# Value tiles turned by SBUF-to-SBUF DMAs and VectorE's 32x32 transposes instead of by TensorE: a gated-delta attention layer with an expert FFN on one core

## The reference, cut to what matters

```python
mixed = hidden_states @ W_qkv
mixed = _causal_conv_silu(mixed.transpose(0, 2, 1), conv_w).transpose(0, 2, 1)
q, k, v = jnp.split(mixed, [KEY_DIM, 2 * KEY_DIM], axis=-1)
...
def step(S, inp):
    qt, kt, vt, gt, bt = inp
    S = S * jnp.exp(gt)[..., None, None]
    v_adj = (vt - jnp.einsum('bhk,bhkv->bhv', kt, S)) * bt[..., None]
    S = S + kt[..., None] * v_adj[..., None, :]
    o = jnp.einsum('bhk,bhkv->bhv', qt, S)
    return (S, o)
```

## Time and profile before

| | us |
|---|---|
| median of 3 runs | 2076.18 |
| lowest and highest | 2070.57, 2081.19 |
| the profiled execution's own time | 2080.1 |
| its span in the trace | 2078.3 |

### The profile page before, as it was taken

One profiled execution on the slowest core, in us unless ns is written; L12 is line 12 of the kernel. 1 busy time (PEld: TensorE's weight loads), 2 busy tenths in 40 slices (PEclk: granted clock), 3 DMA queues, 4 the chain that ended last, 5 costly groups with the idle time before them and its releaser, 6 DMA issues.

```text
span 2078.3 us, 39559 instructions
## 1 busy us (share of the span) xinstructions
PE 2008.6 (97%) x13730; PEld 1713.5 (82%) x13730; DVE 1353.6 (65%) x3169; ACT 909.1 (44%) x2525; POOL 834.1 (40%) x2123
## 2 busy tenths in 40 slices
PE   5789999999999999999999999999999999999999
PEld 3578888888888888888888888888888888887887
DVE  6868877778688878787777445555555444446442
ACT  4555555555465555556555532222223232233221
POOL 1456666666575766666565511100010210101111
PEclk9889999999999999999999999999999999999999
DMA  4233545343535444434443232443334434303441
GB/s 125 51 74 79 97 84 100 79 96 80 89 84 94 92 97 81 97 81 97 88 87 71 77 93 59 94 92 81 77 76 92 118 86 99 69 26 122 152 143 70
DMA packets 388022, 184.25 MB, mean 89 GB/s; under 512 B 249456, under 2 KB 369136, under 8 KB 385776
## 3 DMA queue, kind: packets, MB, share of 16 engines
q1 hardware_dynamic: 354640, 177.73, 37.8%
q10 hardware_dynamic: 33184, 4.01, 1.3%
HBM read 135.26 MB, written 46.40 MB: 87 GB/s over the span
## 4 chain that ended last, share of the span: by engine, by line
PE 69%; issue 10%; DVE 6%; DMA 5%; POOL 4%; ACT 3%; SPq 2%; ACTq 0%; POOLq 0%; DVEq 0%
PE bank L333 17%; PE bank L335 17%; PE bank L334 17%; DMA VT<-v_dram 4%; PE bank L565 3%; PE bank L574 2%; PE bank L548 2%; PE bank L468 2%; PE bank L584 2%; PE bank L556 2%; PE bank L527 2%; PE bank L533 1%; POOL y_out L1823 1%; POOL V L1771 1%; POOL prod L1769 1%
## 5 line engine op out<-in xcount | busy, mean ns | idle before, releaser
L1769 POOL TENSOR_TENSOR prod<-A_in,V 128x60 f32<-128x60 f32 (+24 forms) x992 | 301.4, 304 | 269.6 <-DMA A_in<-a_dram 199.3
L1771 POOL TENSOR_TENSOR V<-V,prod 128x60 f32<-128x60 f32 (+24 forms) x992 | 311.1, 314 | 77.8
L1098 ACT ACTIVATE hid<-bank,bias 128x512 f32<-128x512 f32 x128 | 88.3, 690 | 455.3 <-PE bank L335 453.5
L1813 POOL TENSOR_TENSOR ffn_w_lo<-ffn_raw,ffn_w_hi 128x1024 fp32r<-128x1024 f32 x32 | 77.9, 2437 | 470.3 <-ACT ffn_w_hi L1088 466.4
L1563 DVE TENSOR_TENSOR h_lo<-hid,h_hi 128x512 fp32r<-128x512 f32 x128 | 91.1, 712 | 265.8 <-ACT h_hi L1105 265.8
L1577 DVE SCALAR_TENSOR_TENSOR gate_acc<-bank,rw,gate_acc 128x512 f32<-128x512 f32 x240 | 177.6, 748 | 58.8 <-PE bank L335 58.8
L333 PE MATMUL bank<-ffn_w_hi,h_hi 128*128 128x512 f32 x512 | 199.3, 389 | 1.2 <-DVE h_lo L1563 1.0
L333 PE MATMUL bank<-xn_hi,ffn_w_hi 128*128 128x512 f32 x512 | 200.3, 391 | 0.0
L335 PE MATMUL bank<-xn_hi,ffn_w_lo 128*128 128x512 f32 x512 | 199.2, 389 | 0.0
L334 PE MATMUL bank<-xn_lo,ffn_w_hi 128*128 128x512 f32 x512 | 199.2, 389 | 0.0
L335 PE MATMUL bank<-ffn_w_hi,h_lo 128*128 128x512 f32 x512 | 199.2, 389 | 0.0
(11 more groups left out here) (224 smaller groups left out, 5178.0 us busy)
## 6 DMA issues: line engine op xcount, KB each, us to landing
E<-eg_dram SPq DMA_DIRECT2D x64, 256.0 KB, 8.1
A_in<-a_dram SPq DMA_DIRECT2D x32, 512.0 KB, 4.0
decb<-dec_dram SPq DMA_DIRECT2D x128, 128.0 KB, 4.2
og_dram<-og SPq DMA_DIRECT2D x64, 256.0 KB, 2.2
ffn_raw<-w SPq DMA_DIRECT2D x32, 512.0 KB, 4.0
og_x<-og_dram SPq DMA_DIRECT2D x256, 64.0 KB, 2.7
ogT_dram<-og_y SPq DMA_DIRECT2D x64, 256.0 KB, 2.4
og_in<-ogT_dram SPq DMA_DIRECT2D x16, 1024.0 KB, 5.2
```

The source lines that it names most:

```text
L1098: act.activation(hid[:, i % 2, :], bank[i % 4][:, :], ACT.Gelu_apprx_tanh, bias=bias1[:, k, f * NF + ft:f * NF + ft + 1]).then_inc(S_["gel ...
L1769: pool.tensor_tensor(prod[:, 0:m, 0:n], column, V[:, vb, 0:m, j:j + 1].to_broadcast([P, m, n]), MUL).then_inc(S_["product"], 1)
L1771: pool.tensor_tensor(V[:, vb, 0:m, j + 1:B32], V[:, vb, 0:m, j + 1:B32], prod[:, 0:m, 0:n], ADD).then_inc(S_["solve_step"], 1)
L1813: pool.tensor_tensor(fw[m, "lo", n % 2][:, :], raw[:, i % 2, :], fw[m, "hi", n % 2][:, :].bitcast(f32), SUB).then_inc(S_["ffn_lo"], 1)
```

## The change

TensorE no longer turns the values. `turn_v` on PE (8 transposes in a block) is gone. In its place:

- SP has a new `load_v`, at the end of a step behind its last `decb` load: once both silu tiles of the block are there and the block before has been turned, it issues 16 DMAs from `vS` to a new tile `v_x`, each of 32 partitions x 8 pieces of 32 elements (32 KB). They put the 32x32 blocks of every 128x128 tile at their transposed places.
- DVE has a new `turn_v`: two transposes of 128x512 in 32x32 blocks, from `v_x` to `v_tok`, between `chain_S` of chunk 3 and `convolve(st, "v0")`.
- ACT's `put_v` scales `v_tok` in place. Its two halves move from the middle of the step to its end, around `put_y64`.
- `v_tok` has one buffer instead of two; `v_x` takes the room of the other.
- PE's waits change: `turn_k` waits for what `turn_v(st, 0)` waited for, and `project_v0` waits for the third z gate of the block and no longer for `v_tok`.
- ACT's four carry semaphores become one, each wait still being for its own instruction just before.

```diff
@@ PE
             def project_v0(st):
                 if is_block(st - 1):
-                    pe.wait_ge(S_["v_tok"], 2 * st)
+                    pe.wait_ge(S_["z_gate"], CPS * (st - 1) + 3)
...
             def turn_k(st):
                 b = st - 1
-                pe.wait_ge(S_["v_tok"], 2 * b + 1)
+                if is_block(st):
+                    pe.wait_ge(S_["CP"], CPS * (st + 1))
+                else:
+                    pe.wait_ge(S_["k_rem"], b)
...
@@ PE, attention_step
                     chain_out(st - 2, 1)
-                if turned:
-                    turn_v(st, 0)
...
                 if turned:
-                    turn_v(st, 1)
                     turn_k(st)
@@ ACT
             def put_v(st, half):
                 b = st - 1
-                act.wait_ge(S_["v_turned"], 2 * b + half + 1)
+                act.wait_ge(S_["v_turned"], b + 1)
...
-                    r = act.mul(v_tok[:, b % 2, c, :], TV_BANK[half][:, i * REP * HD:(i + 1) * REP * HD], roots[:, b % 4, c:c + 1])
+                    r = act.mul(v_tok[:, :, c, :], v_tok[:, :, c, :], roots[:, b % 4, c:c + 1])
...
@@ ACT, end of attention_step
                 if turned:
+                    put_v(st, 0)
                     put_y64(st - 1)
+                    put_v(st, 1)
@@ DVE
+            def turn_v(b):
+                dve.wait_ge(S_["v_x"], V_X * (b + 1))
+                if b:
+                    dve.wait_ge(S_["R"], CPS * b)
+                for h in range(REP):
+                    r = dve.transpose(v_tok[:, h, :, :], v_x[:, h * CPS:(h + 1) * CPS, :])
+                r.then_inc(S_["v_turned"], 1)
...
                 if chain:
                     chain_S(st - 2, 3)
+                if turned:
+                    turn_v(st - 1)
                 if now:
                     convolve(st, "v0")
@@ SP
+            def load_v(b):
+                sp.wait_ge(S_["act_v0"], b + 1)
+                sp.wait_ge(S_["act_v1"], b + 1)
+                if b:
+                    sp.wait_ge(S_["v_turned"], b)
+                vf = vS[:, :, :].rearrange("p h t -> p (h t)").rearrange("p (m t) -> p m t", t=P)
+                for to in range(NQD):
+                    for at in range(NQD):
+                        r, q = slice(to * B32, (to + 1) * B32), slice(at * B32, (at + 1) * B32)
+                        sp.dma_start(v_x[r, :, q], vf[q, :, r]).then_inc(S_["v_x"], 16)
...
                 next_decay(3)
+                if turned:
+                    load_v(st - 1)
```

More of the change, by code:

```diff
@@ L191, in build @@
         Y64 = alloc(p2b, "Y64", [NCH, 2 * B32])
-        v_tok = alloc(p2b, "v_tok", [2, CPS, REP * HD])
+        v_tok = alloc(p2b, "v_tok", [REP, CPS, HD])
+        v_x = alloc(p2b, "v_x", [REP * CPS, P])
         z_gate = alloc(p2b, "z_gate", [2, CPS, REP * HD])
@@ L249, in build @@
         KQ_BANK = (WORK_C, WORK_C)
-        TQ_BANK, TK_BANK, TV_BANK = WORK_B, WORK_C, (WORK_C, WORK_B)
+        TQ_BANK, TK_BANK = WORK_B, WORK_C
         def is_block(b):
@@ L316, in build @@
         CONV = 3
+        V_X = 16 * NQD * NQD
         SOLVES = B32 - 1
@@ L487, in turn_k @@
                 i.then_inc(S_["k_turned"], 1)
-            def turn_v(st, half):
-                b = st - 1
-                pe.wait_ge(S_["act_v0"], b + 1)
-                pe.wait_ge(S_["act_v1"], b + 1)
-                if half:
-                    pe.wait_ge(S_["z_gate"], CPS * b + 3)
-                elif is_block(st):
-                    pe.wait_ge(S_["CP"], CPS * (st + 1))
-                elif b:
-                    pe.wait_ge(S_["k_rem"], b)
-                for i in range(2):
-                    c = 2 * half + i
-                    for h in range(REP):
-                        r = pe.transpose(TV_BANK[half][:, (REP * i + h) * P:(REP * i + h + 1) * P], vS[:, h, c * P:(c + 1) * P], C["ident"])
-                r.then_inc(S_["v_turned"], 1)
             def join_y32(b):
@@ L663, in up_part @@
                     pe.wait_ge(S_["z_gate"], CPS * NU)
-                elif k == 0 and i == 1:
-                    pe.wait_ge(S_["v_tok"], 2 * NU)
                 elif k == 0 and i == 2:
@@ L767, in tensor @@
             project_z(1, 1)
-            turn_v(1, 0)
             project_q(1)
             project_z(1, 2)
-            turn_v(1, 1)
             turn_k(1)
@@ L859, in split_weights @@
                 act.copy(w_hi[kind][:, :, part * P:(part + 1) * P], w_raw[:, n % 2, :, :]).then_inc(S_["w_hi"], 1)
+            carries = 0
             def tap(b, kind):
+                nonlocal carries
+                carries += 1
                 gr, sb = b // NSB, b % NSB
@@ L867, in tap @@
                         act.wait_ge(S_[f"act_{kind}"], b)
-                    act.copy(cv[:, 0:KW - 1], C["zero"][:, 0:KW - 1]).then_inc(S_[f"carry_{kind}"], 1)
+                    act.copy(cv[:, 0:KW - 1], C["zero"][:, 0:KW - 1]).then_inc(S_["carry"], 1)
                 else:
                     act.wait_ge(S_[f"act_{kind}"], b)
-                    act.copy(cv[:, 0:KW - 1], cv[:, SB:SB + KW - 1]).then_inc(S_[f"carry_{kind}"], 1)
+                    act.copy(cv[:, 0:KW - 1], cv[:, SB:SB + KW - 1]).then_inc(S_["carry"], 1)
                 act.wait_ge(S_[f"proj_{kind}"], b + 1)
-                act.wait_ge(S_[f"carry_{kind}"], b + 1)
+                act.wait_ge(S_["carry"], carries)
                 act.mul(cv[:, KW - 1:], P_BANK[kind][:, :], taps[:, 4 * gr + n, 0:1]).then_inc(S_[f"tap_{kind}"], 1)
@@ L888, in silu @@
                     if b:
-                        act.wait_ge(S_["v_turned"], 2 * b)
+                        act.wait_ge(S_["v_x"], V_X * b)
                     dst = vS[:, int(kind[1]), :]
@@ L1195, in scalar @@
             put_z(1, 1)
-            put_v(1, 0)
             exponents(3)
@@ L1200, in scalar @@
             put_z(1, 2)
-            put_v(1, 1)
             put_k(1)
@@ L1209, in scalar @@
             rates(3)
+            put_v(1, 0)
+            put_v(1, 1)
             for st in range(2, NU + 2):
@@ L1420, in chain_R @@
                     r = dve.scalar_tensor_tensor(R[:, h, :], bank[K_BANK][:, h * HD:(h + 1) * HD], decay[:, cg, h0 + h:h0 + h + 1],
-                                                 v_tok[:, b % 2, i, h * HD:(h + 1) * HD], MUL, SUB)
+                                                 v_tok[:, h, i, :], MUL, SUB)
                 r.then_inc(S_["R"], 1)
@@ L1688, in vector @@
             gate_series(3)
+            turn_v(0)
             convolve(1, "v0")
@@ L2088, in sync @@
             load_blocks(1)
+            load_v(0)
             sp.wait_ge(S_["rows_out"], 96)
```

13 lines of the change are left out of this document (4 added, 9 removed).

## The result

| | us |
|---|---|
| before, median of 4 runs on the same chip | 2076.03 (2070.57 to 2081.19) |
| after, median of 4 runs | 2258.39 (2244.41 to 2262.26) |
| ratio after / before | 1.0867, 95% interval 1.0812 to 1.0922 |
| span of the profiled execution after | 2254.5 |

The changed kernel is 182 us slower. The forecast had the sign and the place, but 37 us. The mean granted TensorE clock of the span is 0.946, where it was 0.985.

What follows compares the result with a forecast made beforehand. PE, busy 97%, sets the pace, with DVE's convolution close ahead of turn_q. Terms 35 + 10.5 + 3 - 7.7 - 4 = +37 us on the median 2076.18 give 2113 us; range 2080 to 2155.

Steps and rivals of the forecast that it cites:

- The removal: PE without the values' transposes: 0.43 us saved ahead of chunk 3 in 18 steps, 7.7 us (bounds 0 and 12.8).
- DVE's 1.4 us without cover: Two DVE transposes between chain_S of chunk 3 and the v0 convolution make PE late at turn_q: 35 us (29 to 41).
- The waits for `VT`: diagonal's waits for inverses from DRAM, 14.6 us in all: later turn_q removes 4 us (bounds 0 and 14.6).
- the exchange's lateness: v_x reaches DVE 1.5 us late in the 7 steps 0 mod 4 only: 10.5 us.
- The packets' 3.3 us: The exchange's 4096 packets, 13 ns each, take 3.3 us of each DMA engine in a 34 us step.
- Traffic, `og` and `decb` behind the issues: On SP, an og store and two decb loads behind the issues are needed over 10 us later: no cost.
- Rival 1: PE's 28 us gained whole, DVE's part in idle time: 2051, chance 0.06; weaker form 2081, chance 0.11.
- rival 3: VT loads suffer from 4096 more packets: 10 more steps with 2.5 us, +25 us, 2138; chance 0.08.
- The 3 us at the two ends: Delay at both ends of the attention part, block 0 and block 31: 3 us (bounds 0 and 5).
- 0.450 us for an issue, with 7.5 us for 16: SP's price for the 32 KB exchange DMAs, taken from a_dram stores (0.450 us) and VT loads (0.451), with gaps.
- the ordinary step had 2.5 us of room: In step 15 the exchange lands at 611.9 and DVE comes for it at about 614.5: no wait.
- Rival 2: Exchange late in every step at 0.78 us an issue: 95 us instead of 10.5, 2198 (2155 with half the excess); chance 0.15.

Runs made afterwards that it cites:

- x_removed: Changed kernel without the exchange and DVE's transposes, so nothing turns the values and ACT scales vS as it is: 2063.87 us, ratio 0.9962 to before.
- x_noexch: Changed kernel without the exchange DMAs; DVE's two transposes read vS itself, leaving the values' blocks at wrong places: 2101.61 us, ratio 1.0150 to before.
- x_unread: x_noexch with the 16 DMAs issued as in the changed kernel, but DVE reads vS and does not wait for them: 2096.77 us, ratio 1.0129 to before.

## Why the prediction was wrong

**Right, by its own steps.** The removal: 7.7 us forecast, 7.0 measured (`x_removed`). DVE's 1.4 us without cover: 35 us forecast, 37.7 measured (`x_noexch` less `x_removed`), with the two transposes at 1.30 us end to end and `turn_q` idle in each step. `chain_keys` of chunk 2 still starts 0.05 us behind `chain_S` (median, 0.07 before), and at chunk 3 the distance went from 0.51 to 0.08, as forecast. The waits for `VT` fell from 14.6 to 7.2 us, where 4 were expected to go. Without the exchange's lateness the sum says 2102.5, and 2101.6 was measured. The packets' 3.3 us of each DMA engine in a block are borne out: by the pages (37.8% of 2078.3 us before, 39.7% of 2254.5 after) it is 3.4. Traffic, `og` and `decb` behind the issues: nothing forecast, nothing found (`x_unread`). Rival 1 is refuted by `x_removed` (its gain on PE) and `x_noexch` (DVE's idle time as cover), rival 3 by `x_unread`. The 3 us at the two ends were not measured apart.

**The step that failed first: 0.450 us for an issue, with 7.5 us for 16**. I took the price of the a_dram stores and VT loads because size and cutting were alike. Measured: 0.59 at least, 0.61 in the median, 0.73 in the mean, and 12.5 us in the median for 16 (10.8 to 15.5), as here in two steps:

```profile
593.68 13.90 SPq L1930 DMA_DIRECT2D v_x<-vS  x16
...
634.13 11.57 SPq L1930 DMA_DIRECT2D v_x<-vS  x16
```

So the issues took 5 us longer than forecast in the median (3.3 at least), and the ordinary step had 2.5 us of room. The forecast's upper bound of 12.5 us for 16 (0.78 us each) is where the median came out, and nearly half of the blocks took longer. Rival 2's sum of waits was right, then: 95 us against 89.3 measured. I gave this case 0.15 because "the median issue" spoke against it. Two rows spoke for it. Four VT loads in 3.12 us were the nearest to 16 in a row behind `E` and `VT`, and served as a bound only. And the third kind of 32 KB DMA, which I left out, is dearer than the two that I quoted (details of before's line that stores V, ns min/median/max):

```profile
L1916 SPq DMA_DIRECT2D v_dram<-V x66: 516/606/877, 94.8 to 1171.7; - x66
```

0.606 in the median, 0.516 at least. The room of 2.5 us in the ordinary step was worth 0.16 us for each of 16 issues, just the distance from 0.45 to 0.61. Of the 5 us in all, these 0.16 us make 2.6 and the long issues (64 of 512 took over 1 us) make 1.9, the mean of 0.73 less the median. A term with so little room should have been priced by its dearest row, and by a sum of issues and not a median. That the issues "lengthen while the rings are full", as the forecast has it, is shown only so far: the two of 2.99 us fell in a stretch in which the DMA engines' busy share was 1.00 (637 to 640 us, before). How full the rings were no run shows.

**The term that was missing: the granted clock.** Every stall was priced by its own length, in the forecast and in rival 2, which therefore stops at 2198. From 2198 to 2258 it is in the main the half clock behind the stalls: PE busy for 63.8 us more than in `x_noexch` in 28 steps, with the same instructions. It could have been read in the trace of before. There PE stood for over 1.1 us only three times in steps 4 to 31, each time for `diagonal`'s inverses. The longest of them, and the windows around the 2.21 us one (at 399.7):

```profile
541.08 0.21 PE L511 MATMUL bank<-V,CP 32*32 32x32 f32 x1 [3.71 <-DVE V L1401]
```

```profile
396.00:401.30 5.30, 3.08 (x47) 2.45 (x46) 2.92 (x9) 1.81 (x6) 4.25 (x14) 1.00 0.40 105
401.30:404.70 3.40, 3.40 (x60) 3.11 (x60) 1.73 (x4) 1.74 (x5) 2.88 (x7) 0.50 0.41 96
404.70:410.00 5.30, 5.30 (x53) 4.56 (x53) 4.40 (x16) 2.01 (x8) 0.63 (x3) 1.00 0.08 16
```

1.00 with a hole of 2.21 us in it (2.2 of 5.3 us not busy), then 0.50 for 3.4 us in which PE is busy throughout, then 1.00. The three stretches of half clock in these steps begin at 401.3, 541.2 and 1087.3, right behind the three holes (ends at 399.7, 541.1 and 1086.7). So the rows of before said that PE's clock can halve behind a stall of 1.8 us. I had looked at windows of 34 us with 1.00 and stopped there. With it, rival 2 would have stood near 2260, and the range's upper end, 2155, would have looked as narrow as it was.

**The size of the error in these terms.** Each run taken against the kernel before beside it, the 182.4 us are 7.0 of gain by the removal (7.7 forecast), 38.6 for DVE's transposes (34 forecast, 35 + 3 - 4) and 150.7 for the lateness of the exchange (10.5 forecast). By the table above, in the 28 steps, the last is 83 us of standing at `turn_q` (in all 29) and 64 us of slower matmuls.

## What to carry to other kernels

Count the DMAs before the bytes when somebody waits for the last of them: about 0.6 us each on the queue here, and with the long issues between them 10.8 to 15.5 us for 16. Price a stall of TensorE of 1.2 us or more at its length plus, where the clock falls, about 2 us (1.7 to 2.5 here), since the matmuls behind it run at half clock for some us, and look for the few stalls that the trace already has to see it. And before giving work to an engine with idle time, look on which side of its idle time the new work lands: the same two transposes cost 38 us behind `chain_S` and 10 ahead of it.
